# The two ends of a fused gate, filter and masked-convolution kernel: fewer zero products, other rows for GpSimd and tile 0, an earlier lift, four last stores

## What is computed

```python
g  = relu(bn2(einsum('nchw,oc->nohw', x, wg1))).mean(axis=(2, 3))
xg0 = (relu(tanh(g @ wg2.T + bg2)) + beta)[0]          # image 0 alone is used
filt = basis[which frequency each channel gets, by the rounded shares of xg0]   # 96 x 7 x 7
xp = x.reshape(n, c, 7, 8, 7, 8).mean(axis=(3, 5))      # 7 x 7 cells per channel
y  = relu(bn1((xp * filt).sum(axis=(2, 3)) @ w1d[:, :, 1].T + b1d))
x  = x * y[:, :, None, None] + x                         # first layer's output
t  = relu(bn(x.mean(axis=(2, 3)) @ w1.T))
wt = (t @ w2.T + b2).reshape(n * c, 1, 3, 3) * MASK      # four taps: left-up, up, right-up, left
out = depthwise_conv3x3(x, wt) + bias
```

## Time and profile before

| what | us |
|---|---|
| median of three runs | 217.85 |
| the profiled execution | 218.06 |
| its span in the trace | 216.3 |
| busy: TensorE (matmuls) | 206.1 |
| busy: VectorE | 190.1 |
| busy: GpSimd | 171.1 |
| busy: ScalarE | 135.6 |
| DMA | 79.18 MB, 366 GB/s over the span |

### The profile page before, as it was taken

How to read it: one execution, slowest core, us unless ns; L and a number is a source line. 1 busy time by engine, 2 the same in 40 slices (tenths; PEclk the granted TensorE clock), 3 DMA queues, 4 the chain that set the end, 5 groups by cost and what they waited for, 6 DMA issues and landing times.

```text
span 216.3 us, 2655 instructions
## 1 busy us (share of the span) xinstructions
PE 206.1 (95%) x818; PEld 125.6 (58%) x818; DVE 190.1 (88%) x224; ACT 135.6 (63%) x208; POOL 171.1 (79%) x167
## 2 busy tenths in 40 slices
PE   7999999999999999999999999999999999899980
PEld 3557763566555665656665666576557646766540
DVE  3319879997999999999999999999999997989990
ACT  2021025757766867676857685768667888989950
POOL 0202049999999999999999999999999998678870
PEclk9999999999999999999999999999999999999998
DMA  5999999989999999999999999999999367445777
GB/s 152 364 423 434 421 432 419 383 260 376 334 423 421 399 419 432 411 432 422 432 427 422 432 414 429 427 427 432 420 431 397 151 261 295 190 183 225 297 298 297
DMA packets 8382, 79.18 MB, mean 366 GB/s; under 512 B 1040, under 2 KB 1296, under 8 KB 2352
## 3 DMA queue, kind: packets, MB, share of 16 engines
q1 hardware_dynamic: 8208, 78.91, 88.8%
q10 hardware_dynamic: 160, 0.10, 0.2%
HBM read 40.48 MB, written 38.54 MB: 365 GB/s over the span
## 4 chain that ended last, share of the span: by engine, by line
PE 60%; DVE 30%; issue 4%; ACT 3%; ACTq 0%; DVEq 0%
PE banks L911 42%; DVE banks L666 13%; DVE xout L666 6%; DVE xout L675 5%; PE banks L819 3%; PE banks L835 3%; PE banks L896 2%; PE banks L882 2%; ACT banks L746 2%; PE banks L853 2%; PE banks L826 2%; PE banks L884 2%; PE banks L903 2%; DVE stats L554 1%; DVE sums L573 1%
## 5 line engine op out<-in xcount | busy, mean ns | idle before, releaser
L911 PE MATMUL banks<-xin,diag 128*128 128x495 f32 (+4 forms) x480 | 158.8, 483 | 0.8 <-ACT diag L742 0.5
L911 PEld LDWEIGHTS banks<-xin,diag 128*128 128x128 f32 x480 | 87.8, 190 | 55.0 <-issue 37.7
L746 ACT ACTIVATE banks<-xin,wide_sb,coef 128x1008 f32<-128x1008 f32 (+5 forms) x77 | 85.1, 1122 | 18.6 <-DVE xout L675 9.4
L416 POOL TENSOR_TENSOR halves<-xin 128x1568 f32<-128x1568 f32 (+1 forms) x21 | 72.1, 3431 | 21.0 <-DMA xin<-x 21.0
L666 DVE SCALAR_TENSOR_TENSOR banks<-xin,coef,banks 128x1485 f32<-128x1485 f32 (+3 forms) x48 | 81.7, 1702 | 1.5 <-ACT banks L746 0.4
L666 DVE SCALAR_TENSOR_TENSOR xout<-xin,coef,banks 128x1485 f32<-128x1485 f32 (+5 forms) x31 | 41.5, 1358 | 0.6
L421 POOL TENSOR_TENSOR halves<-halves 128x784 f32<-128x784 f32 x18 | 33.2, 1845 | 1.4
L675 DVE SCALAR_TENSOR_TENSOR xout<-xin,coef,banks 128x990 f32<-128x990 f32 (+2 forms) x24 | 29.2, 1215 | 3.0 <-PE banks L911 2.8
L742 ACT ACTIVATE diag<-wide_sb,coef 128x128 f32<-128x128 f32 x72 | 23.4, 389 | 6.6 <-DVE coef L600 6.6
L787 ACT ACTIVATE xout<-banks 128x616 f32<-128x616 f32 (+3 forms) x24 | 16.1, 670 | 15.4 <-PE banks L911 14.8
L426 POOL TENSOR_TENSOR rows<-halves 128x392 f32<-128x392 f32 x18 | 18.3, 1018 | 1.4
(11 more groups left out here) (83 smaller groups left out, 131.0 us busy)
## 6 DMA issues: line engine op xcount, KB each, us to landing
xin<-x SPq DMA_DIRECT2D x23, 1568.0 KB, 10.2
out<-xout SPq DMA_DIRECT2D x23, 1568.0 KB, 12.4
xout<-x SPq DMA_DIRECT2D x3, 392.0 KB, 4.5
xin<-x SPq DMA_DIRECT2D x1, 1120.0 KB, 14.0
out<-xout SPq DMA_DIRECT2D x2, 476.0 KB, 3.5
out<-xout SPq DMA_DIRECT2D x1, 616.0 KB, 3.7
xin<-x SPq DMA_DIRECT2D x1, 448.0 KB, 14.7
wide_sb<-wide SPq DMA_DIRECT2D x1, 435.5 KB, 15.2
```

Source lines behind the costliest of these rows:

```text
L416: eng.tensor_tensor(halves[:, j % 2, first:end, :], cells[:, :, 0, :], cells[:, :, 1, :], ALU.add).then_inc(once_folded, 1)
L746: return sca.activation(acc, above_rows(k, first, end), ACT.Identity, bias=bias[:, k % PER:k % PER + 1], scale=weight(k, UP))
L911: return mm(to, diag[:, k % 2, which, :], grid(k)[:, irows, cols], start=False, stop=(which == LEFT), skip_group_check=True)
```

## The change

It has five parts: one `warm` product less at two places ahead of and behind the gate's products (2 to 1, 3 to 2); GpSimd folds blocks 4 to 6 of tile 0 as well, which VectorE then sums from the fold; tile 0 is split 22/18/16 instead of 20/18/18; `lift_relu` moves in front of `part` on ScalarE; the last tile is stored in four pieces, A, D, P, B, in that order. The numbers of folds waited for go up by one with the added fold.

```diff
-FIRST_ROWS = (20, 18, 18, 0)
+FIRST_ROWS = (22, 18, 16, 0)
...
             k = TILES - 1
-            sp.wait_ge(part_out, AHEAD_FOLD)
             sp.wait_ge(a_out, TILES)
-            store(k, top_a(k), H)
+            store(k, top_a(k), top_p(k))
             sp.wait_ge(d_out, TILES)
             sp.wait_ge(edge_out, TILES)
             store(k, 0, top_b(k))
+            sp.wait_ge(part_out, AHEAD_FOLD)
+            store(k, top_p(k), H)
             sp.wait_ge(b_out, TILES)
             store(k, top_b(k), top_a(k))
             for b in range(OUT_BUFS):
-                parts = 2 if b == k % OUT_BUFS else 0
+                parts = 3 if b == k % OUT_BUFS else 0
...
-            pool.wait_ge(loaded[1], 16)
-            fold_once(1, *FOLDED_1)
+            for j in range(2):
+                pool.wait_ge(loaded[j], 16)
+                fold_once(j, *FOLDED)
...
-            sum_direct(0, 3, 5)
+            sum_direct(0, 3, 4)
             dve.wait_ge(later_mm, 1)
...
-            sum_direct(0, 5, DCT)
+            sum_once_folded(0, 1, *FOLDED)
             sum_array(0).then_inc(cells_done, 1)
             dve.wait_ge(loaded[1], 16)
-            sum_direct(1, 2, FOLDED_1[0])
-            sum_once_folded(1, 1, *FOLDED_1)
+            sum_direct(1, 2, FOLDED[0])
+            sum_once_folded(1, 2, *FOLDED)
...
                 seed_b(k)
+                if t == 1 and g + 1 < NGROUP:
+                    lift_relu(g + 1)
                 if tail(k):
                     part(k)
-                if t == 1 and g + 1 < NGROUP:
-                    lift_relu(g + 1)
                 finish_array(k)
...
             prime(BANK_B)
-            warm(2)
+            warm(1)
             pe.wait_ge(gate_placed, PER)
...
             ins.then_inc(gate_mm, 1)
-            warm(3)
+            warm(2)
             pe.wait_ge(gate_relu, 1)
```

More of the change, by code:

```diff
@@ L47 @@
 ARRAY_CELLS = ((0, 2), (0, 2), (0, 2))
-FOLDED_1 = (4, 7)
+FOLDED = (4, 7)
 ARRAY_AT = (BANK_D * BANK, (BANK_D + 1) * BANK, (BANK_D + 2) * BANK)
@@ L480, in _ @@
                     fold_once(j)
-                    pool.wait_ge(once_folded, j - ONCE[0] + 2)
+                    pool.wait_ge(once_folded, j - ONCE[0] + 3)
                     fold_twice(j)
@@ L559, in sum_ahead @@
                 if j in ONCE:
-                    sum_once_folded(j, j - ONCE[0] + 2).then_inc(cells_done, 1)
+                    sum_once_folded(j, j - ONCE[0] + 3).then_inc(cells_done, 1)
                 else:
```

## The result

| | kernel before | changed kernel |
|---|---|---|
| median of 20 runs each, us | 217.72 (217.19 to 218.36) | 216.28 (215.00 to 218.67) |
| ratio, changed to before | | 0.9914 (0.9897 to 0.9931) |
| profiled execution, us | 218.06 | 218.67 |
| its span, us | 216.3 | 216.9 |

The changed kernel is faster by 0.9% by the ratio, 1.9 us, and by 1.44 us by the medians of all twenty; 216.28 is inside the range of the forecast (214.4 to 216.6). But its executions fall into groups, and the groups go with the mean granted TensorE clock of the core: eleven at 0.992 and above (215.00 to 216.54, median 215.26), two at 0.984 to 0.985 (216.58, 216.76), seven at 0.978 to 0.979 (218.17 to 218.67). The ratio leaves six of the last group out.

A forecast was written before the change was run, and what follows sets the result against it. Bound by a loop of TensorE's taps and VectorE's cell sums, 22.50 us a group and untouched; head 0.55, seed 0.10, rows 0.55, lift 0.25 and stores 1.05 sum to 2.5, so 217.85 goes to 215.35 us, range 214.4 to 216.6.

The forecast's parts named there:

- stores: At the end: four stores, D no longer behind GpSimd's last add, bring 1.05 us (0.5 to 1.5).
- head: Start of the kernel, up to `hide`: 0.55 us (0.4 to 0.6), with `total` at 27.85 instead of 28.24.
- lift: At tile 19: of VectorE's 1.05 us wait for the lift, 0.25 passes, since ScalarE is late next.
- seed of tile 0: Before the first tap: ScalarE's seed of A covers 16 rows instead of 18, worth 0.10 us.
- rows of tile 0: TensorE's taps of tile 0: 12 recorded instructions one row shorter each, worth 0.55 us.
- the part on tile 3: Tile 3's load lands at 26.2 whatever the gate gains; TensorE idles nearly 1 us before `hide`, at no cost.
- Rival 5: At the gate: image 0 lands late, TensorE's step to 2.4 GHz comes later, 221.0 us; 4%.
- Rival 1: At the head: tile 3 lands earlier, the whole gain arrives, 1.5 in place of 0.55, 214.4 us; 7%.
- the gate's products: At the gate: begin in the slot at 6.33, end two slots (0.66 us) earlier; gate brings 0.66 to 1.3.
- The folds: Ahead of the loop: GpSimd's fold of tile 0 costs nothing; `chosen` sooner brings 0.2 us (0 to 0.5).
- Rival 2: In tile 0: VectorE becomes the bound, TensorE's 0.65 doesn't arrive, 216.0 us, or 216.5 with its own taps; 12%.
- rival 4: At the end: each store pays its fixed part alone, stores lose 1.5 us, 217.9, no change; 4%.

The follow-up runs named there:

- e5: The changed kernel once more, no edit: median 217.35 us of twelve executions (215.10 to 219.08), ratio 0.9939 to the kernel before.
- e1: The changed kernel with the two zero products at the gate put back (`warm` 2 and 3): 216.06 us, ratio 0.9926 to the kernel before.
- e4: The changed kernel with the last tile's three stores of before put back: ratio 0.9942 to the kernel before.
- e3: The changed kernel with one more zero product of 512 columns between `mix(0)` and `hide(0)`: 215.88 us, ratio 0.9919 to the kernel before.
- e2: The kernel before with only the two zero products at the gate taken out: ratio 1.0043, slower.
- e11: e7 with the last tile's three stores of before: 216.42 us, ratio 0.9928 to the kernel before.
- e7: e6 with tile 0 split 21/18/17 instead of 22/18/16: 215.38 us, ratio 0.9890 to the kernel before.
- e9: The kernel before without the zero product between `mix(0)` and `hide(0)`, gate untouched: 219.16 us against 218.00, ratio 1.006.
- e6: The changed kernel with `total_step(0)` ahead of tile 3's sum in VectorE's queue: 215.73 us, ratio 0.9919 to the kernel before.
- e8: e6 with `lift_relu` behind `part` again, as before the change: 215.78 us, ratio 0.9904 to the kernel before.
- e10: e7 with the last tile in three stores, D, then A and P together, then B: 215.94 us, ratio 0.9906 to the kernel before.
- e12: e7 with ScalarE's wait for GpSimd's folds before tile 18's scaled copy reduced by one: 215.16 us, ratio 0.9874 to the kernel before.

## Why the prediction was right, and where it was wrong

**The sum, where the clock holds, came out: 215.26 against 215.35.** Its terms did not all, and that they meet within 0.1 is partly luck: the stores brought 0.43 less than forecast, the head (as what is left) 0.29 and the lift 0.11 more. That the median of all twenty, 216.28, lies in the range is luck too: nine executions had lost the clock at some point, which no term allows for, and in e5, where eight of twelve had, the median was 217.35.

| term | forecast | measured | from |
|---|---|---|---|
| head | 0.55 | 0.84 as what is left of 217.72 - 215.26 (no trace shows it); 0.43 in e1's trace, 1.67 in e4's | landing of tile 3 and end of the gate |
| seed of tile 0 | 0.10 | 0.10 | e1 |
| rows of tile 0 | 0.55 | 0.54 | e1, e4 |
| lift | 0.25 | 0.36 | changed, e1, e3, e4 against before |
| stores | 1.05 | 0.62 | last tap's end to last landing, 3.88 to 3.90 in eight traces with four stores, 4.49 to 4.51 in five with the old three |

**The step that failed** is in the part on tile 3: "now TensorE stands idle for nearly 1 us there", which was priced at nothing. The place and the length were right (0.92), the price was not. I had ruled it out by one row, "TensorE kept its fast slots over the 0.49 us wait before the first tap", but behind that wait came long taps, and behind this hole come products of 4 and 16 columns. (That these small products matter is inferred: in e2 a hole of 0.89 ahead of products of 392 columns did nothing. No run fills the stretch behind the hole with large ones.)

Rival 5 named the mechanism, the clock, and looked for it at the gate. There it did not happen: image 0 was late in e2's trace, TensorE had a hole of 0.89 us before the gate's products, and they were fast at once; the gate's sum came at 13.33. The place of the first step, which one trace could not show, varies far more than the half microsecond that the prediction quotes: the weight loads are short (0.19 us for 0.34) from 4.67 on in e11, and in e7 still long at 6.98.

What falls is the stretch behind tile 3's hole, in 17 of the 32 executions of the changed kernel (fifteen were at full clock), and it costs 1.2 to 1.5 us in four of the five whose mean clock reads 0.984 or 0.985 (3.1 in the fifth) and about 3 where it reads 0.977 to 0.979. The price can be followed in the profiled execution: `total` to coefficients 3.89 us (3.49 in e1), coefficients to first tap 3.04 (1.85), first tap to tile 2's end 25.93 (25.06), 2.46 in all. In e2's trace the same three stretches lose 3.86 against the kernel before.

The Trainium skill, "TensorE: Matmul & The Clock Gate", section "HAM oscillation", describes a kernel that loses its clock by waiting 3 to 5 us for a DMA at each tile. Here a hole of 0.69 us followed by small products was enough (e9), so the absence of long waits did not make the head safe; the measurement decides.

**The head.** Its reasoning held: VectorE was there at 25.03 and waited 1.51 for tile 3. But 26.2 was taken as a constant, and it is not: in fourteen traces tile 3 lands between 24.41 and 27.77. Nor is the gate's end: with the trimmed gate the `gate_sum` product starts between 12.61 (e5) and 13.58 (e7). Wherever VectorE doesn't wait for tile 3 ahead of it, `total` starts 13.56 or 13.57 behind that product (e1, e3, e4, e6 to e8, e10 to e12). So the hole comes where tile 3 is late against the gate, not late as such: in e5 tile 3 landed at 25.74, half a microsecond before it did in the kernel before, and the hole was 0.78, since the gate had ended early.

Rival 1, given 7%, is therefore not another way for the kernel to go, but one end of what each execution draws. The working had a slip too: with one product less the gate's products would by its own numbers begin in the slot at 6.33, one slot earlier than at 6.87 and not two, which is 0.33 less than it counts. The folds brought 0.13, not 0.2. Behind the load neither made a difference.

**Tile 0.** Rival 2 fell: VectorE caught up, as the earlier trace rows had suggested. Only when e6 gave it a sum more to do in tile 0 was it late, by 0.30.

**The lift.** As argued, ScalarE is late next, and the 1.05 did not pass whole. That no wait for GpSimd was on the chain held for the changed kernel's trace; with a head 1.2 us faster (e6, e7) it no longer did, and in e4, the changed kernel's head with tile 3 early, ScalarE already waits 0.27 there.

**The stores.** That the bytes queued set the end held, and rival 4 fell: P lands 0.6 behind D, not 1.8. The size was off because I started the queue at D's issue, as if A were out of it by then. The landings read otherwise: tile 22's store at 212.42, A at 213.13, D at 214.58, P at 215.20, B at 216.40 (issue and time to landing added). At D's issue, 211.30, tile 22's store was still in the queue and all of A behind it. The four pieces, 1606 KB, follow that landing without a break in 3.98 us, 403 GB/s; before it was 4.60 (211.20 to 215.80). B lands 3.85 behind its issue, for a forecast of 3.3 to 3.6. The difference is the 0.62. Before, nothing moved from 210.50 to 211.20 (DMA share 0.00); now the share is 0.57 from 211.00 to 211.60 and 0.93 in the 0.4 us after that, so little more is left in it. P alone moved slower, 196 KB (201 in the prediction's units) in 0.62 us, about 320 GB/s. The Trainium skill, "DMA: Bandwidth & Descriptors", section Bandwidth, would have pieces batched to 1 MiB or more for 75% of peak; four pieces of 0.2 to 0.6 MB, queued behind one another, moved at 403 GB/s here and ended 0.6 us sooner than three, so for pieces queued at the end of a kernel the runs disagree with it. No store of 1 MiB was tried in their place.

**Open.** Why tile 3 lands where it does in an execution, no run here tells. It isn't shown either whether the changed kernel's executions at full clock had no hole, like e4's, or had one and kept the clock: no trace shows it at full clock. What sets the depth of the fall (0.984 or 0.978) is open too. And e12 and the changed kernel were each compared with the kernel before, not with one another.

## What to carry to other kernels

Before pricing a gain at nothing because a load hides it, look at what the engine that now waits is: for TensorE a hole of 0.7 to 0.9 us in a stretch of small products cost 1.2 to 3.9 us, up to four times the hole. Mend it at its cause, by moving the work that TensorE waits for ahead of the load in its engine's queue (e6), rather than by a filler, which costs when the load is early (e3). And where a change gives its gain in some executions only, group the executions by granted clock before reading a median.

## What was not expected of the hardware

The clock fell from 2.4 to 1.2 GHz 0.2 to 2.3 us behind a hole of 0.69 to 0.92 us and stayed there for about 3 us (e9), 7 us (changed) and 10 us (e2). A hole of 0.89 before the gate's large products, in e2, did nothing. One execution of the kernel before, which has no such hole in its trace, also took 222.46 us at a mean clock of 0.968. And one load of 1.6 MB, issued between 6.5 and 7.2 us in each trace behind the same loads, landed anywhere within 3.4 us (24.41 in e4, 27.77 in e7).
